# A fused cross-attention and feed-forward kernel: another order of the head, other warm-up products, and a tail with F(6) in halves

## The reference, cut to what matters

```python
# x, ctx: (16, 128, 256); mask: (16, 128); all weights 256 x 256, fp32
def attn(q, c, mask):
    Q = q @ Wq.T + bq
    K = c @ Wk.T + bk
    s = where(mask, -inf, Q @ K.T)             # one head of 256
    return softmax(s) @ c @ Wo.T + bo          # the values are the context itself
def ffn(x):
    y = x @ sign(W).T * scale + bias           # sign: +1 where W >= 0, else -1
    return clip(y, -100, 100)
x = x + tanh(g_xattn) * attn(layernorm(x), ctx, mask)
x = x + tanh(g_ffn) * ffn(layernorm(x))        # eps 1e-5 in both
```

## Time and profile before

| | |
|---|---|
| median of 3 runs | 83.41 us (83.16 to 85.63) |
| the profiled execution's own time | 82.64 us |
| its span, first to last instruction | 80.9 us |
| PE busy | 68.2 us, 84% of the span |
| DVE, POOL, ACT busy | 58.8, 53.1, 44.5 us |
| chain that ended last, by engine | PE 64%, DMA 13%, DVE 8%, SP's queue 6%, ACT 4% |

### The profile page before, as it was taken

How to read it: one execution, slowest core, us unless ns; L and a number is a source line. 1 busy time by engine, 2 the same in 40 slices (tenths; PEclk the granted TensorE clock), 3 DMA queues, 4 the chain that set the end, 5 groups by cost and what they waited for, 6 DMA issues and landing times.

```text
span 80.9 us, 1584 instructions
## 1 busy us (share of the span) xinstructions
PE 68.2 (84%) x507; PEld 63.1 (78%) x507; DVE 58.8 (73%) x185; ACT 44.5 (55%) x118; POOL 53.1 (66%) x108
## 2 busy tenths in 40 slices
PE   2977869936999999999999999999999999985200
PEld 2965659924999899989999998999999899744100
DVE  0038369373494797999799989979967996269990
ACT  0602094749189729936980995498289714713000
POOL 5400434899849758995998699589959077965420
PEclk9999999999999999999999999999999999999855
DMA  2799933999930000030003002100300040030123
GB/s 11 217 308 282 316 138 135 356 369 349 329 120 0 0 8 4 0 129 9 0 0 130 0 0 91 47 0 0 130 0 0 2 129 7 0 134 0 40 93 127
DMA packets 8288, 8.10 MB, mean 100 GB/s; under 512 B 596, under 2 KB 8152, under 8 KB 8280
## 3 DMA queue, kind: packets, MB, share of 16 engines
q1 hardware_dynamic: 7664, 7.47, 28.2%
q10 hardware_dynamic: 552, 0.53, 2.1%
q0 software_dynamic: 64, 0.00, 0.1%
HBM read 5.90 MB, written 2.10 MB: 99 GB/s over the span
## 4 chain that ended last, share of the span: by engine, by line
PE 64%; DMA 13%; DVE 8%; SPq 6%; ACT 4%; issue 2%; DVEq 0%
PE ps_Z L557 13%; DMA x_sb<-in_x_dram 13%; PE ps_K L557 12%; PE ps_O L628 9%; PE ps_F L557 8%; PE ps_S L557 8%; PE ps_xT L552 8%; PE ps_cT L552 3%; ACT p_sb L210 2%; PE ps_S L620 2%; DVE y_clip L455 1%; SPq L141 1%; SPq L144 1%; DVE y_scaled L446 1%; DVE x_sb L423 1%
## 5 line engine op out<-in xcount | busy, mean ns | idle before, releaser
L199 ACT ACTIVATE K_sb<-ps_K,u_col 128x256 f32<-128x256 f32 x16 | 6.7, 470 | 14.2 <-PE ps_K L557 14.2
L321 POOL TENSOR_TENSOR xb_sb<-x_sb,bo_g 128x256 f32<-128x256 f32 x16 | 11.4, 733 | 0.6
L326 POOL TENSOR_TENSOR y_biased<-y_scaled,bias_g 128x256 f32<-128x256 f32 x14 | 10.0, 736 | 2.5 <-DVE y_scaled L467 2.5
L557 PE MATMUL ps_K<-cT_hi,wqk_hi 128*128 128x256 f32 x32 | 10.4, 325 | 0.8 <-DVE wqk_lo L496 0.8
L557 PE MATMUL ps_Z<-woT_hi,cT_hi 128*128 128x256 f32 x32 | 9.8, 305 | 0.0
L557 PE MATMUL ps_Z<-woT_hi,cT_lo 128*128 128x256 f32 x32 | 9.0, 282 | 0.0
L557 PE MATMUL ps_K<-cT_lo,wqk_hi 128*128 128x256 f32 x32 | 9.0, 282 | 0.0
L557 PE MATMUL ps_K<-cT_hi,wqk_lo 128*128 128x256 f32 x32 | 9.0, 282 | 0.0
L557 PE MATMUL ps_Z<-woT_lo,cT_hi 128*128 128x256 f32 x32 | 9.0, 282 | 0.0
L189 ACT ACTIVATE xn<-x_sb,nmr_x,rstd_x 128x256 f32<-128x256 f32 x16 | 8.8, 607 | 0.0
L557 PE MATMUL ps_F<-wT,x1T_hi 128*128 128x256 f32 x30 | 8.1, 303 | 0.8 <-DVE x1T_lo L439 0.8
(11 more groups left out here) (114 smaller groups left out, 196.4 us busy)
## 6 DMA issues: line engine op xcount, KB each, us to landing
ctx_sb<-in_ctx_dram SPq DMA_DIRECT2D x8, 256.0 KB, 7.6
x_sb<-in_x_dram SPq DMA_DIRECT2D x8, 256.0 KB, 7.7
out_dram<-out_sb SPq DMA_DIRECT2D x7, 256.0 KB, 2.5
wk_sb<-in_L_xattn_Wk_dram ACTq DMA_DIRECT2D x1, 256.0 KB, 4.3
wq_sb<-in_L_xattn_Wq_dram SPq DMA_DIRECT2D x1, 256.0 KB, 4.0
wo_sb<-in_L_xattn_Wo_dram ACTq DMA_DIRECT2D x1, 256.0 KB, 7.2
mask_u<-in_mask_BxS_bk_dram SPq DMA_DIRECT2D x1, 256.0 KB, 7.9
w_sb<-in_L_ffn_weights_dram SPq DMA_DIRECT2D x1, 256.0 KB, 8.1
```

The lines of the kernel that those rows point to most:

```text
L199: nc.scalar.activation(K_sb[:, g % 2, m], ps_K[:, m], ACT.Identity, bias=u_col[:, m:m + 1]).then_inc(K_done, 1)
L321: nc.gpsimd.tensor_tensor(xb_sb[:, r], x_sb[:, r], bo_g[:], ALU.add).then_inc(xb_done, 1)
L326: nc.gpsimd.tensor_tensor(y_biased[:, g % 2, b], y_scaled[:, g % 2, b], bias_g[:, 0], ALU.add).then_inc(biased_done, 1)
L557: last = nc.tensor.matmul(dst, lhsT, rhs, start=(n == 0), stop=(n == len(pairs) - 1))
```

## The change

In the head: the warm-up is six products of zeros and two more behind the bias vectors; Wk is loaded by SP, second; the gates are loaded by ACT, ahead of Wo; the order of SP's other loads changes; the folded weights are made in two banks (those of the scores) and are copied and split by halves; K(0) is put in two banks; xn(0) is made by POOL and xT(0) copied by DVE; scores, P^T and O of group 0 come before K(1) with the transpose of ctx(1) ahead of them, and the sign weights' transpose moves into group 1. In the tail: exp(7) comes before the copy of Z(7) on ACT; F(6) is made in halves between O and the transposes of x1 of group 7; group 6 is biased by DVE, clipped by POOL and added by DVE; all of group 7's bias is DVE's.

```diff
-WARM_UP = 18
+WARM_UP = 6
...
+        ps_wqk = [s[:, 0:D] for s in s_banks]
+        ps_K0 = [ps_K[:, 0], f_bank[:, 0:T]]
...
                 sp.dma_start(ctx_sb[:, rows(g), :], ctx_rows[:, rows(g), :]).then_inc(ctx_loaded[g], 16)
 
             sp.dma_start(wq_sb[:], wq.rearrange("(c p) d -> p c d", p=P)).then_inc(wq_loaded, 16)
+            sp.dma_start(wk_sb[:], wk.rearrange("(c p) d -> p c d", p=P)).then_inc(wk_loaded, 16)
             load_ctx(0)
             load_x(0)
-            load_x(1)
             load_ctx(1)
             sp.dma_start(mask_u8[:], mask.rearrange("(o b) k -> o b k", o=1).to_broadcast([P, B, P])
                          ).then_inc(mask_loaded, 16)
+            load_x(1)
+            sp.dma_start(bo_sb[:], bo.rearrange("(o d) -> o d", o=1).to_broadcast([P, D])).then_inc(bo_loaded, 16)
             sp.dma_start(w_sb[:], w_ffn.rearrange("(c p) d -> p c d", p=P)).then_inc(w_loaded, 16)
-            sp.dma_start(bo_sb[:], bo.rearrange("(o d) -> o d", o=1).to_broadcast([P, D])).then_inc(bo_loaded, 16)
+            load_x(2)
+            load_ctx(2)
             sp.dma_start(scale_sb[:], scale_ffn.rearrange("(o d) -> o d", o=1).to_broadcast([P, D])
                          ).then_inc(scale_loaded, 16)
             sp.dma_start(bias_sb[:, 0, :], bias_ffn.rearrange("(o d) -> o d", o=1).to_broadcast([P, D])
                          ).then_inc(bias_loaded, 16)
-            for g in range(2, G):
+            for g in range(3, G):
...
-            act.dma_start(wk_sb[:], wk.rearrange("(c p) d -> p c d", p=P)).then_inc(wk_loaded, 16)
...
+            for k, v in enumerate((g_xattn, g_ffn)):
+                act.dma_start(gates[:, k:k + 1], v.rearrange("(o d) -> o d", o=1).to_broadcast([P, 1])
+                              ).then_inc(gates_loaded, 16)
             act.dma_start(wo_sb[:], wo.rearrange("(c p) d -> p c d", p=P)).then_inc(wo_loaded, 16)
...
-            evict_cT_hi(0)
             act.wait_ge(gates_loaded, 32)
             nc.scalar.activation(tanh_g[:], gates[:], ACT.Tanh).then_inc(tanh_ready, 1)
-            act.wait_ge(ps_wqk_ready, 1)
-            nc.scalar.copy(wqk_hi[:], ps_K).then_inc(wqk_hi_ready, 1)
+            evict_cT_hi(0)
+            for m in range(DC):
+                act.wait_ge(ps_wqk_ready, m + 1)
+                nc.scalar.copy(wqk_hi[:, m], ps_wqk[m]).then_inc(wqk_hi_ready, 1)
             act.wait_ge(ps_woT_ready, 1)
             act.wait_ge(tanh_ready, 1)
             nc.scalar.activation(woT_hi[:], by_chunk(z_bank), ACT.Identity, scale=tanh_g[:, 0:1]).then_inc(woT_hi_ready, 1)
-            normalise_x(0)
             act.wait_ge(u_ready, 1)
-            evict_K(0)
-            evict_xT(0)
+            for m in range(DC):
+                act.wait_ge(ps_K0_ready, m + 1)
+                nc.scalar.activation(K_sb[:, 0, m], ps_K0[m], ACT.Identity, bias=u_col[:, m:m + 1]).then_inc(K_done, 1)
+            evict_cT_hi(1)
+            normalise_x(1)
+            exp(0)
+            evict_PT(0)
             evict_Z(0)
-            for i in range(G + 1):
-                if 1 <= i < G:
+            evict_xT(1)
+            for i in range(1, G + 1):
+                if i < G:
                     evict_K(i)
-                if 1 <= i < G:
+                if i < G:
                     evict_x1T_hi(i - 1)
-                elif i == G:
+                else:
...
-                if 1 <= i < G:
+                if i < L:
                     evict_Z(i)
-                if i < G:
                     exp(i)
+                elif i == L:
+                    exp(i)
+                    evict_Z(i)
                 if i + 1 < G:
...
-                if i == 0:
+                if i == 1:
...
+            def clip(g):
+                for b in range(GB):
+                    if g == L - 1:
+                        pool.wait_ge(dve_biased_done, 1)
+                    else:
+                        pool.wait_ge(biased_done, GB * g + b + 1)
                     nc.gpsimd.tensor_scalar(y_clip[:, g % 2, b], y_biased[:, g % 2, b], lim[:, 0:1], lim[:, 1:2],
                                             ALU.min, ALU.max).then_inc(pool_clip_done, 1)
...
             norm_of_x(0)
+            pool.wait_ge(nmr_x_done, 1)
+            for b in range(GB):
+                nc.gpsimd.tensor_scalar(xn[:, b], x_sb[:, b], rstd_x[:, b:b + 1], nmr_x[:, b:b + 1],
+                                        ALU.mult, ALU.add).then_inc(xn_done, 1)
...
-            for i in range(G + 1):
+            for i in range(G):
...
-                if 1 <= i < G:
+                if i >= 1:
                     rstd_of_x1(i - 1)
-                    if i == L:
-                        pool.wait_ge(lim_ready, 2)
-                        clip_and_add(L - 2)
-                elif i == G:
-                    for b in range(GB):
-                        rstd_of_last_x1(b)
-                    add_last_bias(1)
...
+                if i == 0:
+                    fold_affine()
+            pool.wait_ge(lim_ready, 2)
+            clip(L - 2)
+            add_x1(L - 2)
+            for b in range(GB):
+                rstd_of_last_x1(b)
+            clip(L - 1)
...
+                dve.wait_ge(dve_biased_done, b + 2)
...
+            stats_x(0)
             split_cT(0)
-            stats_x(0)
-            dve.wait_ge(wqk_hi_ready, 1)
-            nc.vector.tensor_tensor(wqk_lo[:], ps_K, wqk_hi[:].bitcast(F32), ALU.subtract).then_inc(wqk_lo_ready, 1)
+            for m in range(DC):
+                dve.wait_ge(wqk_hi_ready, m + 1)
+                nc.vector.tensor_tensor(wqk_lo[:, m], ps_wqk[m], wqk_hi[:, m].bitcast(F32), ALU.subtract
+                                        ).then_inc(wqk_lo_ready, 1)
+            dve.wait_ge(ps_u_ready, 1)
+            nc.vector.tensor_copy(u_col[:], ps_u).then_inc(u_ready, 1)
             dve.wait_ge(woT_hi_ready, 1)
...
-            dve.wait_ge(ps_u_ready, 1)
-            nc.vector.tensor_copy(u_col[:], ps_u).then_inc(u_ready, 1)
+            dve.wait_ge(xT_prod, 1)
+            nc.vector.tensor_copy(xT[:, 0], ps_xT).then_inc(xT_done, 1)
             stats_x(1)
+            mask_and_min(0)
+            split_cT(1)
...
+            residual(0)
+            stats_x1(0)
...
+            stats_x(2)
+            for i in range(1, G):
+                if i >= 2:
...
-                if i + 2 < G:
+                if 2 <= i < G - 2:
                     stats_x(i + 2)
-                if i >= 1:
-                    split_x1T(i - 1)
-                if i < G:
-                    mask_and_min(i)
+                split_x1T(i - 1)
+                mask_and_min(i)
                 if 2 <= i < L:
                     clip_and_add(i - 2)
                 if i + 1 < G:
                     split_cT(i + 1)
-                if i >= 1:
+                if i == 1:
+                    stats_x(3)
+                if i < L:
                     scale_y(i - 1)
...
             aggregate_last_x1(0)
             stats_last_x1(1)
+            scale_y(L - 1)
             split_last_x1T(0)
             aggregate_last_x1(1)
             split_last_x1T(1)
-            clip_and_add(L - 1)
+            dve.wait_ge(scaled_done, GB * L)
+            nc.vector.tensor_tensor(y_biased[:, (L - 1) % 2], y_scaled[:, (L - 1) % 2], bias_g[:].to_broadcast([P, GB, D]),
+                                    ALU.add).then_inc(dve_biased_done, 1)
             for b in range(GB):
                 scale_last_y(b)
...
+            dve.wait_ge(pool_clip_done, 2 * GB)
+            nc.vector.tensor_tensor(out_sb[:, rows(L - 1)], y_clip[:, (L - 1) % 2], x1_sb[:, rows(L - 1)], ALU.add
+                                    ).then_inc(out_done, 1)
             for b in range(GB):
+                r = L * GB + b
+                dve.wait_ge(scaled_done, r + 1)
+                nc.vector.tensor_tensor(y_biased[:, L % 2, b], y_scaled[:, L % 2, b], bias_g[:, 0], ALU.add
+                                        ).then_inc(dve_biased_done, 1)
                 clip_and_add_last(b)
...
-                    last = accumulate(ps_K[:, m], pairs)
-                last.then_inc(K_prod, 1)
+                    last = accumulate(ps_K[:, m] if g >= 1 else ps_K0[m], pairs)
+                    if g == 0:
+                        last.then_inc(ps_K0_ready, 1)
+                if g >= 1:
+                    last.then_inc(K_prod, 1)
...
+                if GB - 1 in batches:
+                    last.then_inc(F_prod, 1)
...
                 for b in range(GB):
+                    ffn(L - 1, [b])
                     pe.wait_ge(x1_done, GB * L + b + 1)
...
+            pe.wait_ge(zeros_ready, 1)
+            for _ in range(WARM_UP):
+                nc.tensor.matmul(f_bank[:, 0:P], zeros[:], zeros[:], start=True, stop=True)
...
             nc.tensor.transpose(ps_vec, vec_rows[:], ident[0:2 * DC, 0:2 * DC]).then_inc(ps_vec_ready, 1)
+            for _ in range(2):
+                nc.tensor.matmul(f_bank[:, 0:P], zeros[:], zeros[:], start=True, stop=True)
...
```

(33 more changed lines are left out.)

76 lines of the change are left out of this document (30 added, 46 removed).

## The result

The changed kernel has a median of **89.4 us** (88.54 to 90.35, 4 runs) against 83.75 for the kernel before (83.16 to 85.63, 4 runs): ratio 1.061, 95% interval 1.046 to 1.076, slower. The forecast was 86.8, range 83.8 to 89.5, so 89.4 lies just inside. It is near what the rival with the falling clock gave for both stalls, 89.5, but in the profiled execution the clock fell in one of them only. That execution took 88.54 (span 86.7), 5.90 more than the one of before.

The account below looks back on a forecast made before the run. TensorE was taken as the bound between attend(0) and the last group, with head and tail chains around it. 82.64 + 2.6 (attend(1) late) + 1.1 (tail) = 86.35, plus half of the median's 0.77 offset: 86.8 us, range 83.8 to 89.5.

Parts of the forecast that it names:

- the rival with the falling clock: Clock drops in the emptier waits before attend(0) and ffn(0): 1.7 us per fall, 88.5 or 89.5 for both; 28%.
- the forecast's own band: The main case, in which the forecast itself holds: 85.3 to 88.0 us, chance 42%.
- the step from the profiled execution to the median: Whole kernel: the runs' median stood 0.77 us above the profiled execution; the forecast added half of that.
- K(0) at 10.85: Head: K(0)'s first product starts at 10.85, behind Wo's landing and transposes, 0.75 us earlier; bounds 9.5 to 11.6.
- The bytes ahead stay the same: Head: moving Wk to SP's queue leaves the bytes ahead of ctx(0) and x(0), so their landings were left unchanged.
- K(0) to attend(0), 8.3: Head: a chain through x(1)'s statistics, POOL and ACT ahead of exp(0) takes 8.3 us; attend(0) at 19.15, 0.87 earlier.
- attend(0) to attend(1), 10.7: Group 1: x(2)'s late statistics delay xn(2), exp(1) and wT; 10.7 us instead of 7.24, attend(1) 2.6 late.
- attend(1) to group 7, nothing: Middle groups: same PE order and work, PE the bound, so nothing more is gained or lost.
- The tail, +1.1: Tail: scale_y(6), group 6's bias and POOL's clip delay the last additions by 1.1 us; bounds -0.5 to +1.6.
- the loads come early: Head: Wq and Wo may land earlier, so K(0) starts earlier and the kernel is no slower than can be told; 17%.
- The stall does not form: Group 1: no wait after attend(0), because a link of the chain was misread; 81.7 to 83.3 us, chance 13%.

Follow-up runs that it names:

- g4: The changed kernel with Wk's load back at the head of ACT's queue, the gate loads still on ACT: 89.47 us, ratio 1.083 to the kernel before.
- e4: The changed kernel with exp(0), P^T(0) and Z(0) ahead of normalise_x(1) on ACT, P^T(0) and O(0) ahead of x(1)^T on PE: 87.84 us.
- e1: The changed kernel with the statistics of x(2) moved on DVE from behind w_mid to ahead of the sign weights: 88.28 us.
- h1: The changed kernel with the edits of e1, e4 and g2 together: 83.74 us, ratio 1.018 to the kernel before.
- h4: The kernel before with x(2)'s statistics behind those of x1(0) on DVE, and x(3)'s behind the split of ctx(2): 83.79 us.
- e2: The changed kernel with eight products of zeros on PE ahead of transpose_p(1): 90.03 us, ratio 1.091 to the kernel before.
- g2: The changed kernel with eight products of zeros behind the bias vectors instead of two: 88.56 us, ratio 1.072 to the kernel before.
- t1: The kernel before with all of the new tail and nothing else of the change: 84.97 us, ratio 1.018.
- t2: The kernel before with only exp(7) put ahead of Z(7)'s copy on ACT: 83.53 us, ratio 1.013.
- h3: h1 with the tail of the kernel before, exp(7) still ahead of Z(7)'s copy: 82.69 us, ratio 0.996 to the kernel before.
- h2: The kernel before with x(2)'s statistics behind mask_and_min(0) and the split of ctx(1) on DVE, exp(7) ahead of Z(7)'s copy: 81.14 us.

## Why the prediction came out as it did

The direction and the mechanism were right and the size fell short: the median missed by 2.6 and left the forecast's own band, 85.3 to 88.0; only the rival's price kept it in the range. Of the 2.6, 0.4 is the step from the profiled execution to the median (0.86, of which I gave about half). The other 2.2 were missing between 86.35 and 88.54, point by point:

- **K(0) at 10.85:** measured 10.86, by other means. Wo landed at about 8.9, not 9.39; ctx(0) and x(0), whose landings I left as they were, came 0.8 and 2.1 later, and DVE held the low part of the weights behind x(0). "The bytes ahead stay the same" was the failing step: the bytes do, the queue doesn't (g4).
- **K(0) to attend(0), 8.3:** 8.98. The chain was the one named (e4 took it away and 2.4 us went); most links were a little longer, POOL's third small operation above all, 0.45 in place of 0.2, and the copy of x(0)^T began 0.3 late.
- **attend(0) to attend(1), 10.7:** 11.37, and 10.56 in the execution whose clock stayed up. The links, from DVE's late statistics to wT, are all in the rows, and e1, h1 and h4 show them from three sides. The rival "the clock falls in the new stalls", to which I gave 28%, is what happened in the second stall: 1.5 us, 0.8 here and the rest behind attend(1). Its price for one fall, 1.7, was near; for both it asked 2.7 and reached 89.5, so that 89.4 lies beside it is chance.
- **attend(1) to group 7, nothing:** +1.00. 0.6 of it is the clock (41.39 in e2). 0.4 is in every kernel with the new order, clock or not (41.4 for 41.0), 0.2 of it in the first group; why stays open. With both statistics late on DVE h4 lost 1.07 here, and h1, which has those of x(3) at the same place, only this 0.4, so it isn't their place alone.
- **The tail, +1.1:** +0.94, made up of -0.35 and +1.29. DVE waited 0.61 for POOL's clip, as foreseen.

The rival "the loads come early" was right on Wq (1.0 earlier) and Wo and failed on ctx(0) and x(0). "The stall does not form" fell outright; its times, 81.7 to 83.3, also leave out the 0.4 that the others have for the step to the median. What I underrated is the chance of the falling clock. The changed kernel, e1, e4, g2 and g4 each had a low stretch in or right behind one of the two stalls; of the five traces with the old head two had one (t1, t2), and of e2, h1 and h3, where a filler or the edits took idle time out, none. The Trainium skill (TensorE: Matmul & The Clock Gate, Why this matters for your kernels) has idle gaps between bursts bring back the low clock. The fall in the changed kernel agrees, behind 1.09 us of work in 3.27; the same wait before attend(0) in the kernel before, with 1.20 in 3.20, had none, and in t1 and t2 it had one.

Not tried: the new head with all loads on their old queues, the parts of the new tail one by one, and h2's order of DVE with the longer zero warm-up.
